# A factorization-machine tower on one core: another split pair in layer 2, rows copied a tile ahead, indices loaded per block

## What is computed

```python
x0 = xk = e                                  # [1024, 39, 16]
for idx, (W, b) in enumerate(params):        # W: [39, fk, 128], fk = 39, 64, 64
    z = relu(einsum('bhd,bkd,hks->bsd', x0, xk, W) + b[None, :, None])
    if idx != 2:
        xk = z[:, :64, :]
        direct.append(z[:, 64:, :])
    else:
        direct.append(z)
logit = sum(concatenate(direct, axis=1), axis=-1)
h = concatenate([logit, dense_ctx], axis=1)
h = relu(h @ W_top1 + b_top1)
h = relu(h @ W_top2 + b_top2)
y = h @ W_top3
```

## Time and profile before

| what | value |
|---|---|
| timed runs, median of 3 | 1306.11 us (1290.72, 1306.11, 1309.57) |
| the profiled execution's own time | 1279.85 us |
| its span, first to last instruction | 1278.0 us |
| mean granted TensorE clock | 0.995 of full |
| TensorE busy | 1220.3 us, 95% of the span |
| VectorE busy | 1102.7 us, 86% |
| GpSimd busy | 909.5 us, 71% |
| ScalarE busy | 666.2 us, 52% |
| DMA | 233.56 MB, 183 GB/s |

### The profile page before, as it was taken

The page is one execution under the profiler, slowest core; times in us unless marked ns, Lnnn a source line. Parts: engine busy times, 40 slices in busy tenths (PEclk is TensorE's granted clock), DMA queues, the critical chain, the costliest instruction groups (busy, mean ns, idle before and its releaser), DMA issues.

```text
span 1278.0 us, 15260 instructions
## 1 busy us (share of the span) xinstructions
PE 1220.3 (95%) x4050; PEld 766.0 (60%) x4050; DVE 1102.7 (86%) x995; ACT 666.2 (52%) x708; POOL 909.5 (71%) x581
## 2 busy tenths in 40 slices
PE   0679999999999999999999999999999999999999
PEld 0345666666666666666666666666666666666653
DVE  1258999989999899989999899999999899999980
ACT  0234555555555555556555465556555565555542
POOL 6677788787878778787878778787878755555530
PEclk9989999999999999999999999999999999999999
DMA  7198888888987878889888878889888888898500
GB/s 193 22 236 183 194 200 197 199 203 211 215 180 185 189 190 206 196 204 221 193 180 191 195 192 201 199 210 221 181 181 191 194 196 200 195 218 208 129 15 0
DMA packets 134532, 233.56 MB, mean 183 GB/s; under 512 B 16434, under 2 KB 23715, under 8 KB 134401
## 3 DMA queue, kind: packets, MB, share of 16 engines
q1 hardware_dynamic: 83053, 151.03, 50.7%
q10 hardware_dynamic: 41474, 79.71, 24.2%
q0 software_dynamic: 9984, 2.58, 2.5%
HBM read 229.39 MB, written 6.23 MB: 184 GB/s over the span
## 4 chain that ended last, share of the span: by engine, by line
PE 91%; DMA 4%; POOL 3%; DVE 1%; issue 1%; ACT 0%; SPq 0%; DVEq 0%; POOLq 0%; ACTq 0%
PE z_odd L909 36%; PE z_even L909 34%; PE z_even L943 8%; PE z_odd L943 7%; POOL gathered L496 2%; DMA x_shift<-x_rows 1%; PE whole_psum L937 1%; DMA x_rep<-x_rows 1%; DMA x_rows<-xt_and_ctx 1%; PE x_even L963 1%; PE x_odd L963 1%; PE z_odd L877 1%; PE x_even L937 1%; PE x_odd L937 1%; DVE whole L753 0%
## 5 line engine op out<-in xcount | busy, mean ns | idle before, releaser
L509 POOL TENSOR_TENSOR rest<-whole,head 128x1024 fp32r<-128x1024 f32 x256 | 610.7, 2397 | 244.0 <-ACT head L620 241.3
L753 DVE TENSOR_TENSOR whole<-x_banks,x_rep 128x1024 f32<-128x1024 f32 x480 | 567.2, 1212 | 49.4 <-ACT x_banks L578 42.5
L620 ACT CAST head<-whole 128x1024 fp32r<-128x1024 f32 x256 | 268.6, 1050 | 187.4 <-DVE whole L753 122.9
L496 POOL DMA_INDIRECT gathered<-in_tbl,idx x312 | 296.9, 952 | 84.5 <-issue 77.0
L620 ACT CAST head<-whole_psum 128x1024 fp32r<-128x1024 f32 x160 | 162.2, 1014 | 123.3 <-DVE whole_psum L753 118.1
L909 PE MATMUL z_odd<-whole,w_whole 128*128 128x512 f32 x468 | 217.1, 592 | 0.5 <-DVE whole L753 0.5
L753 DVE TENSOR_TENSOR whole_psum<-x_banks,x_rep 128x1024 f32<-128x1024 f32 x160 | 196.1, 1226 | 15.0 <-DMA x_rep<-x_rows 13.4
L786 DVE TENSOR_TENSOR rest<-whole_psum,head 128x1024 fp32r<-128x1024 f32 x160 | 194.6, 1216 | 14.0 <-ACT head L620 14.0
L909 PE MATMUL z_even<-whole,w_whole 128*128 128x512 f32 x428 | 198.5, 592 | 0.0
L909 PE MATMUL z_odd<-head,w_rest 128*128 128x512 f32 x393 | 190.6, 485 | 7.0 <-POOL rest L509 5.2
L909 PE MATMUL z_even<-head,w_rest 128*128 128x512 f32 x375 | 178.6, 476 | 0.3 <-POOL rest L509 0.3
(11 more groups left out here) (94 smaller groups left out, 924.0 us busy)
## 6 DMA issues: line engine op xcount, KB each, us to landing
x_rep<-x_rows SPq DMA_DIRECT2D x128, 512.0 KB, 11.1
x_rep<-x_rows ACTq DMA_DIRECT2D x128, 512.0 KB, 11.8
x_shift<-x_rows SPq DMA_DIRECT2D x93, 546.0 KB
x_rep<-x_rows SPq DMA_DIRECT2D x32, 384.0 KB
x_rep<-x_rows ACTq DMA_DIRECT2D x32, 384.0 KB
x_rep<-x_rows SPq DMA_DIRECT2D x32, 256.0 KB
gathered<-in_tbl,idx POOLq DMA_INDIRECT x312, 7.5
x_rows<-xt_and_ctx SPq DMA_DIRECT2D x32, 78.0 KB
```

The lines of the kernel that those rows point to most:

```text
L496: nc.gpsimd.indirect_dma_start(gathered[:, f, :], None, tables[f], bass.IndirectOffsetOnAxis(ap=idx[:, f:f + 1], axis=0)).then_inc(s_gathe ...
L509: nc.gpsimd.tensor_tensor(rest[:, split_slot(product)], whole_slot(product), head[:, split_slot(product)].bitcast(F32), ALU.subtract).then ...
L620: nc.scalar.copy(head[:, split_slot(product)], src).then_inc(s_head, 1)
L753: nc.vector.tensor_tensor(out[0:rows, 0:width, :], xk[0:rows, :].unsqueeze(1).to_broadcast([rows, width, N]), x0, ALU.mult).then_inc(s_pro ...
```

## The change

- `KINDS`: in layer 2 the ninth pair becomes V (was U) and the third becomes P (was V). In layer 1 the second becomes P and the third V (the other way round before).
- `GATHERS_AFTER` for layer 2: (0, 2, 2, 2) for the four P pairs, was (2, 2, 2) for three. For layer 1 unchanged.
- The copy of the gathered rows to `emb` (`spread`) moves from the middle of a block's first transposes to the end of layer 2 of the tile before (`EMB_AFTER`); `next_direct` moves one head earlier (`D0_AFTER`).
- `idx_all` goes. SyncE loads each block's indices into `idx` by a DMA of their own (`next_indices`), after it has waited for the copy to `emb`.
- In tile -1, SyncE stores tile 1's rows first and then loads x_rep of tile 0.
- SyncE and ScalarE run one turn fewer in the loop and have its tiles written out.

```diff
--- before.py
+++ after.py
@@ -29,16 +29,16 @@
 
 
 
-KINDS = {1: "UVPPUPVPVP", 0: "UUUU", 2: "UUVUPUVPUP"}
+KINDS = {1: "UPVPUPVPVP", 0: "UUUU", 2: "UUPUPUVPVP"}
 ORDER = (1, 0, 2)
 EARLY_OUT = (0, 2, 3) + (4,) * PAIRS
 SPLITS = {layer: len(kinds) - kinds.count("U") for layer, kinds in KINDS.items()}
 PE_ORDER = {1: (0, 1, 2, 3, 4, 5, 6, 7, 8, 9), 2: (0, 1, 2, 3, 4, 5, 6, 7, 8, 9)}
 WHOLE_SLOTS = 6
 SPLIT_SLOTS = 4
-GATHERS_AFTER = {1: (0, 1, 0, 0, 8), 2: (2, 2, 2)}
+GATHERS_AFTER = {1: (0, 1, 0, 0, 8), 2: (0, 2, 2, 2)}
+GATHERS_EARLY = (20, 10, 9)
 GATHERS_OF_TILE = (10, 10, 11, 8)
-GATHERS_EARLY = (20, 10, 9)
 D2_AFTER = 6
 XT_AFTER = 3
 X1_AFTER = 2
@@ -49,7 +49,8 @@
 LOADS = 5
 CPL = CHUNKS // LOADS
 TWICE = 2
-D0_AFTER = 5
+EMB_AFTER = 6
+D0_AFTER = 4
 AHEAD = 2
 WARM_UP = 34
 FILL_UP = 10
@@ -145,7 +146,6 @@
         wt3 = sb("wt3", [P, M2])
         ctx_rows = sb("ctx_rows", [P, BLOCKS, CTX])
 
-        idx_all = sb("idx_all", [P, BLOCKS, FIELDS], I32)
         idx = sb("idx", [P, FIELDS], I32)
         gathered = sb("gathered", [P, FIELDS, DIM])
         emb = sb("emb", [P, SPC, FIELDS * DIM])
@@ -210,8 +210,7 @@
         s_ring = sem("ring_ready")
         s_first = sem("first_rows_copied")
         s_select = sem("first_shift_selected")
-        s_ids = sem("ids_loaded")
-        s_idx = sem("idx_ready")
+        s_idx = sem("idx_loaded")
         s_gather = [sem(f"gather_landed_{g}") for g in range(len(GATHER_GROUPS))]
         s_emb = sem("emb_ready")
         s_x0 = sem("x0_transposed")
@@ -394,7 +393,16 @@
         @block.sync
         def _(sp):
 
-            sp.dma_start(idx_all[:], ids.rearrange("(b p) f -> p b f", p=P)).then_inc(s_ids, 16)
+            by_block = ids.rearrange("(b p) f -> b p f", p=P)
+            sp.dma_start(idx[:], by_block[0]).then_inc(s_idx, 16)
+
+            def next_indices(t):
+
+                done = t.plus(AHEAD).blocks(1, 1)
+                if t.first % TPB == TPB - AHEAD and (t.turn is not None or done < BLOCKS):
+                    sp.wait_ge(s_emb, done)
+                    rows = by_block[done] if t.turn is None else by_block[bass.ds(done, 1)]
+                    sp.dma_start(idx[:], rows).then_inc(s_idx, 16)
 
             sp.dma_start(w0_k[:, 0:FIELDS, :], w0).then_inc(s_w0_ext, 16)
             sp.dma_start(w0_k[:, FIELDS:, :], w0[:, 0:XROWS - FIELDS, :]).then_inc(s_w0_ext, 16)
@@ -455,19 +463,23 @@
 
             def body(t):
                 first = has_layer0(t) and not has_layers12(t)
-                if has_layer0(t):
-
-                    load_rep(t, range(LOADS if first else TWICE))
+                if has_layer0(t) and not first:
+
+                    load_rep(t, range(TWICE))
+                next_indices(t)
                 if has_transposes(t):
                     nxt = t.plus(AHEAD)
                     row = x_rows[nxt.count(1)] if nxt.turn is None else x_rows[bass.ds(nxt.count(1), 1)]
                     wait(sp, s_xt, nxt.count(1, 1))
                     now = xt[:, nxt.first % 2, :]
                     sp.dma_start(source(row, 0, [[N, FIELDS], [1, N]]), now).then_inc(s_stored, 16)
-                    if has_layer0(t):
+                    if not first and has_layer0(t):
                         sp.wait_ge(s_prod, before(t, 0, PAIRS0))
                     sp.dma_start(source(row, FIELDS, [[N, XROWS - FIELDS], [1, N]]),
                                  now[0:XROWS - FIELDS, :]).then_inc(s_stored, 16)
+                    if first:
+                        load_rep(t, range(LOADS))
+                        sp.wait_ge(s_prod, before(t, 0, PAIRS0))
                     wait(sp, s_stored, nxt.count(32, 32))
                     for r in range(SPC if has_layer0(t) else 0):
                         src = source(row, r, [[N, FIELDS], [SPC * N, CHUNKS0], [1, N]])
@@ -475,7 +487,7 @@
                 if has_layer0(t) and not first:
                     load_rep(t, range(TWICE, LOADS))
 
-            steps(sp, body)
+            steps(sp, body, TURNS - 1)
 
             sp.wait_ge(s_prod, before(Tile(TILES - 2), 2, PAIRS))
             sp.dma_start(wt1, W_top1[0:2 * P].rearrange("(c p) m -> p c m", p=P)).then_inc(s_wt, 16)
@@ -486,11 +498,6 @@
 
         @block.gpsimd
         def _(pool):
-            def new_indices(b):
-
-                src = idx_all[:, b, :] if isinstance(b, int) else idx_all[:, bass.ds(b, 1), :]
-                nc.gpsimd.tensor_copy(idx[:], src).then_inc(s_idx, 1)
-
             def gather(f):
 
                 nc.gpsimd.indirect_dma_start(
@@ -515,18 +522,14 @@
                 while layer == 2 and fields:
                     gather(fields.pop(0))
 
-            pool.wait_ge(s_ids, 16)
-            new_indices(0)
-            pool.wait_ge(s_idx, 1)
+            pool.wait_ge(s_idx, 16)
             for f in range(FIELDS):
                 if f == FIELDS // 2:
                     pool.wait_ge(s_ident0, 1)
                     nc.gpsimd.affine_select(out=ident[:], in_=ident[:], compare_op=ALU.not_equal, fill=1.0,
                                             base=0, pattern=[[-1, P]], channel_multiplier=1).then_inc(s_ident, 1)
                 gather(f)
-            pool.wait_ge(s_emb, 1)
-            new_indices(1)
-            pool.wait_ge(s_idx, 2)
+            pool.wait_ge(s_idx, 32)
             early = list(range(FIELDS))
             for f in early[:GATHERS_EARLY[0]]:
                 gather(f)
@@ -548,9 +551,7 @@
                     if k == 0:
                         def refill():
 
-                            pool.wait_ge(s_emb, ahead.blocks(1, 1))
-                            new_indices(ahead.blocks(1, 1))
-                            pool.wait_ge(s_idx, ahead.blocks(1, 2))
+                            pool.wait_ge(s_idx, ahead.blocks(16, 32))
                 rests(t, 1, fields, refill)
                 rests(t, 2, fields)
 
@@ -629,14 +630,20 @@
                     wait(act, s_sum2, t.blocks())
                 relu_by_sample(direct2, t, z_of(t, 2)[:], bias[:, 2:3]).then_inc(s_d2, 1)
 
+            def spread(t):
+
+                wait_gathers(act, t, range(len(GATHER_GROUPS)))
+                wait(act, s_x0, t.count(1))
+                nc.scalar.copy(emb[:], gathered[:].rearrange("p f d -> p (f d)").unsqueeze(1)
+                               .to_broadcast([P, SPC, FIELDS * DIM])).then_inc(s_emb, 1)
+
+            def next_block_starts(t):
+
+                first = t.plus(AHEAD + 1)
+                return first.first % TPB == 0 and (first.turn is not None or first.first < TILES)
+
             def transposed(t):
                 nxt = t.plus(AHEAD)
-                if nxt.first % TPB == 0:
-
-                    wait_gathers(act, nxt, range(len(GATHER_GROUPS)))
-                    wait(act, s_x0, nxt.count(1))
-                    nc.scalar.copy(emb[:], gathered[:].rearrange("p f d -> p (f d)").unsqueeze(1)
-                                   .to_broadcast([P, SPC, FIELDS * DIM])).then_inc(s_emb, 1)
                 act.wait_ge(s_x0, nxt.count(1, 1))
                 wait(act, s_stored, nxt.count(32, -32))
                 nc.scalar.copy(xt[:, nxt.first % 2, :],
@@ -670,6 +677,8 @@
 
             def body(t):
                 if not has_layers12(t):
+                    if not has_layer0(t):
+                        spread(Tile(0))
                     if has_transposes(t):
                         transposed(t)
                     if not has_layer0(t):
@@ -689,13 +698,15 @@
                 for n in range(SPLITS[2] + 1):
                     if n == X1_AFTER and has_layer0(t):
                         next_x1(t)
+                    if n == EMB_AFTER and next_block_starts(t):
+                        spread(t.plus(AHEAD + 1))
                     if n == D0_AFTER and has_layer0(t):
                         next_direct(t)
                     if is_last(t):
                         for job in range(EARLY_OUT[n], EARLY_OUT[n + 1]):
                             mlp_out(job)
                     heads(t, 2, start=n, upto=n + 1, loads={6: [2], 7: [3], 9: [4]} if has_layer0(t) else {})
-            steps(act, body)
+            steps(act, body, TURNS - 1)
             out_layer2(Tile(TILES - 1))
             for n in range(early_jobs, len(mlp_jobs)):
                 mlp_out(n)
```

## The result

| | before | after |
|---|---|---|
| median, timed side by side (20 runs each) | 1304.31 us (1281.73 to 1310.99) | 1310.66 us (1306.49 to 1314.79) |
| profiled execution | 1279.85 us, span 1278.0 | 1310.71 us, span 1308.9 |
| ratio after / before, 95% interval | | 1.0153 (1.0126 to 1.0180) |

The ratio takes of each kernel only the executions within 1.5% of its fastest, which leaves out much of the wide spread of before; by all runs' medians the change costs 6.4 us, 0.5%, and profile against profile 30.9 us. Three numbers so far apart need an explanation, and it comes from experiment 1. The forecast was 1324.0 us, and no change that can be told by 2%.

The account below looks back on a forecast made before the run. TensorE was taken as the bound, never waiting in a steady tile. Terms -11.7 + 31.6 - 2 = +17.9 us, added to the runs' median 1306.11, gave 1324.0 us; own range 1308 to 1334, 8-in-10 range 1291 to 1340.

Parts of the forecast that it names:

- Part 2: Layer 2's third pair: its rest, now GpSimd's, waits behind eight gathers and delays TensorE, +31.6 us (bounds 31.6 and 39.1).
- signs of being wrong: Layer 2 on TensorE one 14.9 us piece despite gathers, VectorE or x_rep loads as releasers there, or tiles above 37.6 us.
- Part 1: Layer 2's ninth pair: splitting it saves TensorE 0.36 us a tile, -11.7 us over 32 tiles.
- its equations: TensorE's layers 1 and 2: u + 47f = 12.44, 5u + 29f = 15.28, giving split matmul 0.228 us, unsplit pair 1.73.
- Part 3: Block starts: rows copied a tile ahead, per-block index loads landing at 748, wanted at 750.6; both hidden, worth 0.
- rival (c): Block's index load lands 5 us later, delaying GpSimd 2.4 us in six tiles: 14 us, 1338; chance 0.06.
- 0.23 us for seven gathers: Layer 2's third pair in tiles with seven gathers: rest 0.52 us late, 0.23 lost, 1.4 us in six tiles.
- Part 4: The start: storing rows before x_rep loads lets x_shift be asked some 12 us earlier; -2 us, bounds 0 and -5.
- sum of +17.9 us: Whole kernel: -11.7 + 31.6 - 2 us, giving 1297.8 us on the profiled execution of 1279.85.
- adding the sum to 1306.11: Whole kernel: the same 17.9 us put on the shown runs' median, 2.1% above the profile, giving 1324.0 us.
- (a): Layer 2's third pair: its rest is ready in time, the saving comes through whole, -13.7 us, 1292.4; chance 0.16.
- (b): GpSimd bounds more than one place, eighth pair's rest also late: 13 us more, 1337, or 1350; chance 0.14.

Follow-up runs that it names:

- experiment 1: The kernel before, unchanged, run and profiled again: 1302.19 us.
- 6: Changed kernel plus only a pad of 32 unused bytes per partition ahead of the index tile: 1304.36 us, ratio 1.0034 to the kernel before.
- 9: Changed kernel plus the 32-byte pad and the index load on ScalarE's queue, third pair's rest still on GpSimd: 1312.02 us, ratio 1.0236.
- 3: Changed kernel with layer 2's third pair's rest back on VectorE and its gathers (2, 2, 2), ninth pair's split kept: 1290.03 us, ratio 0.9906.
- 10: Changed kernel with 32-byte pad, index load on ScalarE's queue, third pair's rest on VectorE, layer 2 gathers (2, 2, 2): 1278.75 us, ratio 0.9934.
- Experiment 4: Changed kernel with the pair kinds and gathers of before, keeping the new start, earlier row copy and per-block indices: 1303.18 us, ratio 0.9962.
- 5: Same kernel as 10 with fewer executions (4 in place of 12): 1281.05 us, ratio 0.9832.
- 2: Changed kernel with six gathers ahead of layer 2 instead of eight, the others moved to other rests: 1300.98 us, ratio 1.0110.

## Why the prediction came out as it did

**The deciding step was right, in place, order and size** (Part 2). The third pair's rest starts behind the eighth gather; the lateness returns in each tile with gathers; a part of 0.3 us is hidden. Its term was 31.6 us; 28.6 us was measured in the changed kernel (1.38 us a tile) and 1.48 us a tile (37.30 - 35.82) in 6 and 9, against 1.51. That it is a bit less in the changed kernel fits the wider distance of the matmuls, though no run tried this alone: TensorE comes to the third pair later after pair 5 of layer 1, the event that starts GpSimd's work. Experiments 3 and 10 take the rest away from GpSimd, leave the gathers as they are, and the wait is gone. One of the forecast's signs of being wrong came up, tiles above 37.6 us (seven, 37.73 to 38.57): they are the first one and those at or behind an index load, not plain ones.

**The mis-sized term is the split** (Part 1): -11.7 forecast, -0.8 measured. The step that failed is its equations' silent assumption that a matmul of a split pair keeps the 0.228 us of before. It became 0.233, over 82 of them a tile, and gave back what the split saved. Nothing in the trace of before could show this; the diff could have raised the question, as it drops a buffer of 1248 bytes allocated ahead of the heads and rests. Experiment 4 shows the loss without the split, 6 gives it back with 32 bytes.

**Part 3 was wrong on the index load.** It was costed at nothing, "hidden by 2 us and more", with 11.1 us to land. The DMA issues of the changed kernel (count, KB, median us to landing), its chain and the timelines of ScalarE and GpSimd say otherwise, beside the earlier trace rows:

```profile
idx<-in_ids SPq DMA_DIRECT2D x8, 19.5 KB, 13.9
...
309.43 15.66 DMA idx<-in_ids
...
322.12 1.06 ACT L621 CAST head<-whole 128x1024 fp32r<-128x1024 f32 x1 [0.39 <-PE z_odd L920]
...
325.23 2.37 POOL L516 TENSOR_TENSOR rest<-whole,head 128x1024 fp32r<-128x1024 f32 x1 [3.54 <-DMA idx<-in_ids]
```

The load was issued at 309.43 and landed at 325.09. The head for that rest was ready at 322.12 + 1.06 = 323.18, so 13.8 us after the issue the indices were wanted: the margin was the forecast's (750.6 - 736.5 = 14.1). What failed is the landing time, 15.66 us here and 13.6 to 15.7 in the six loads of the loop, where the forecast took the 11.1 of the loads ahead. So the mechanism of rival (c) took place, and this rest started 2.0 us late. But its price was some 3.5 us and not 14, as two tiles only were hit in earnest (37.96 and 37.07, rests 2.0 and 1.1 us late); two more rests were 0.2 to 0.3 us late and two in time. The Trainium skill, DMA: Bandwidth & Descriptors, section on queues, rings and completion order, says that each DMA engine consumes one queue's descriptors in ring order, and that the two issuing engines have rings of their own. The traces agree with the first: a load of 19.5 KB behind two large ones on SyncE's queue took 13.6 to 15.7 us, and 1.74 with nothing ahead. On ScalarE's queue (experiments 5, 9 and 10), where x_rep loads were ahead as well, it landed 10.7 to 13.3 us after its issue, by the updates of its semaphore, and was wanted after 14.8 to 16.7, so no rest waited; what the other queue gives and what the earlier issue isn't told apart.

The copy to `emb` shows no cost in its new place, as forecast: with the index load moved away, the six tiles that hold it are 36.07 to 36.12 us in experiment 9, where the forecast's 0.23 us for seven gathers on top of 35.82 makes 36.05.

**Part 4 gave little.** The second store no longer holds the x_shift load, as forecast, but the load was asked for only 6.4 us earlier and then took 23.05 us, where it had taken 17.24, and TensorE still waited 1.34 us for layer 0 of tile 1. SyncE's queue, the chain (of before, then of the changed kernel), and TensorE of the changed kernel, beside the earlier trace rows, and a stretch of the start (columns as in the earlier trace rows):

```profile
61.49 0.33 SPq L478 DMA_DIRECT2D x_rows<-xt_and_ctx  x1
...
76.64 1.25 SPq L486 DMA_DIRECT2D x_shift<-x_rows  x3
...
83.86 17.24 DMA x_shift<-x_rows
...
77.48 23.05 DMA x_shift<-x_rows
...
101.89 6.28 PE L954 MATMUL z_even<-whole,w0s 117*128 117x512 f32 x14 [1.34 <-DVE whole L764]
...
62.00:82.00 20.00, 20.00 (x30) 7.43 (x30) 3.58 (x5) 1.71 (x3) 15.12 (x17) 0.57 1.04 271
```

In this stretch TensorE was granted 0.57 of its clock, so mostly the lower level, where the profile of before has 0.92. The start gave -0.6 us, with the end -1.0, and not -2.

**That the number came out 1% off is in part luck.** The sum of +17.9 us was 13.0 too low against the profiles (1297.8 forecast, 1310.71 measured), and the base 1306.11 lay 26.3 above the profile that the sum was made on, so the forecast was 13.3 too high on the median (1324.0 against 1310.66): two errors of opposite sign. The step that failed besides the split is adding the sum to 1306.11. By experiment 1 that median of before contains a standstill in the start, which the changed kernel's runs mostly don't have. The prediction saw that its profile lay 2.1% below the median and took it for spread that both kernels would share.

**The rivals.** (a), the saving comes through whole, fell: no tile with gathers is without the wait. (b), GpSimd bound in more than one place, isn't what the changed kernel shows in its plain tiles, but 2 shows that it is near. (c) took place at a quarter of its price.

## What to carry to other kernels

When a step is given to another engine, look first at what stands ahead of it in that engine's order, and compare the end of that work with the time at which the result is wanted; the busy share (71% here) doesn't show it. When an edit drops or resizes a buffer, compare a piece of work that the edit doesn't touch, as layer 1 here: if its time moved, look at where the data lie before blaming the new code. For a small load that something waits for, take the landing time that loads in its place on the queue show, and issue it with room to spare: 19.5 KB took 1.7 us with nothing ahead and 13.6 to 15.7 behind two large loads. And before a sum is put on a median, see whether the profiled execution has the same start as the runs of the median; a second profile of the same kernel showed it here.

## What the runs showed of the hardware

- Matmuls of split pairs stood 0.233 us apart with their operands moved by an odd multiple of 32 bytes (1248 and 224 were tried), and 0.228 to 0.229 in the old place and with a move by 192; an unsplit pair stayed at 1.72 us.
- A load of 19.5 KB took 1.74 us to land at the program's start and 13.6 to 15.7 us in the six of the loop, behind two x_rep loads on one queue. The chain's row of the first one in the changed kernel:

```profile
0.74 1.74 DMA idx<-in_ids
```

- When TensorE came late to the first split pair behind unsplit ones, by 1.67 and 1.79 us, 0.28 to 0.30 us of it was made up: the next matmul followed after 0.33 to 0.35 us in place of 0.63.
- In some executions TensorE, VectorE and ScalarE stood still for 10 to 29 us right after the first transposes (10.45 in experiment 4, 12.14 in 5, 28.70 in 1); the tiles behind it are as ever. The cause is open.
